# Output projection moved from a stage of its own into the attention loop of a Trainium2 kernel

## What is computed

```python
scores = jnp.einsum('bhqd,bhkd->bhqk', q, k) * scale
scores = jnp.where(causal[None, None], scores, -jnp.inf)
att = jax.nn.softmax(scores, axis=-1)
y = jnp.einsum('bhqk,bhkd->bhqd', att, v)
y = y.transpose(0, 2, 1, 3).reshape(b, t, c)
return y @ Wc                    # the output projection, 256 x 256
...
x = x + _L0_attn_ref(xn, ...) + _L0_ffn_ref(xn, ...)
```

## Time and profile before

| | us |
|---|---|
| median of 3 runs | 2054.63 (2052.05 to 2055.58) |
| profiled execution | 2050.78 |
| its span in the trace | 2049.0 |
| attention's last copy of `pv` ends | 1923.0 |
| `project_out`'s first load issued | 1929.78 |
| last addition ends | 2045.45 |

### The profile page before, as it was taken

The page is one execution under the profiler, slowest core; times in us unless marked ns, Lnnn a source line. Parts: engine busy times, 40 slices in busy tenths (PEclk is TensorE's granted clock), DMA queues, the critical chain, the costliest instruction groups (busy, mean ns, idle before and its releaser), DMA issues. The chain is left out here.

```text
span 2049.0 us, 42600 instructions
## 1 busy us (share of the span) xinstructions
PE 1939.1 (95%) x14289; PEld 733.6 (36%) x14289; DVE 1795.2 (88%) x4744; ACT 1578.8 (77%) x2078; POOL 359.0 (18%) x618
## 2 busy tenths in 40 slices
PE   7899999999699999999999999999999999999698
PEld 6455555555222222222222222222222222222165
DVE  5699999999889999999999989999999999997187
ACT  2566666666089999999899989999999999999500
POOL 0112221111112121221212212122121221211000
PEclk8999999999589999999999999999999999999889
DMA  4133333325411230311303113031130321300376
GB/s 165 42 89 94 99 97 102 86 87 126 91 28 23 32 54 2 54 30 26 54 2 54 31 24 54 2 54 32 24 54 2 53 38 18 54 2 13 101 211 206
DMA packets 146213, 123.32 MB, mean 60 GB/s; under 512 B 82068, under 2 KB 132668, under 8 KB 144572
## 3 DMA queue, kind: packets, MB, share of 16 engines
q1 hardware_dynamic: 137324, 112.55, 25.3%
q10 hardware_dynamic: 8720, 8.65, 1.4%
HBM read 69.50 MB, written 50.86 MB: 59 GB/s over the span
## 5 line engine op out<-in xcount | busy, mean ns | idle before, releaser
L1051 ACT ACTIVATE prob<-st 128x1024 f32<-128x1024 f32 (+3 forms) x1280 | 1071.7, 898 | 83.3 <-PE st L1170 75.4
L1183 PE MATMUL pv<-prob,V 128*32 128x512 f32 (+3 forms) x5120 | 598.6, 542 | 0.1
L1146 PE MATMUL sm<-K,Q 48*128 48x512 f16 (+3 forms) x2176 | 542.1, 350 | 17.0 <-DVE pm L1109 4.7
L1094 DVE CUSTOM_DVE_ANT_0 sm<-sm,mask 128x128 f32<-128x128 f32 (+3 forms) x1024 | 490.5, 510 | 61.1 <-PE sm L1146 53.7
L1109 DVE TENSOR_REDUCE pm<-sm 128x1 f32<-128x512 f32 x768 | 494.6, 685 | 15.0 <-PE sm L1146 12.6
L1170 PE MATMUL st<-Q,K 50*128 50x512 f16 (+3 forms) x2560 | 472.5, 353 | 21.5 <-ACT prob L1051 10.9
L1009 POOL TENSOR_SCALAR_AFFINE_SELECT prob<-prob 128x256 f32<-128x256 f32 x512 | 206.1, 409 | 1116.5 <-ACT prob L1051 1111.4
L1146 PEld LDWEIGHTS sm<-K,Q 48*128 48x128 f16 x2176 | 173.8, 94 | 392.6 <-DVE pm L1109 156.6
L1105 DVE CUSTOM_DVE_ANT_0 sm<-sm,excess 128x512 f32<-128x512 f32 x384 | 264.8, 716 | 25.5 <-PE sm L1146 16.2
L1170 PEld LDWEIGHTS st<-Q,K 50*128 50x128 f16 x2560 | 125.3, 93 | 408.5 <-ACT prob L1051 321.7
L1044 ACT ACTIVATE excess<-st 128x1024 f32<-128x1024 f32 x188 | 190.4, 1032 | 5.1 <-DVE pm L1105 0.7
(11 more groups left out here) (151 smaller groups left out, 1896.2 us busy)
## 6 DMA issues: line engine op xcount, KB each, us to landing
Q<-scratch_q SPq DMA_DIRECT2D x102, 128.0 KB, 4.0
K<-scratch_k SPq DMA_DIRECT2D x102, 128.0 KB, 6.2
x<-in_x SPq DMA_DIRECT2D x18, 512.0 KB, 4.5
scratch_v<-Vs SPq DMA_DIRECT2D x64, 128.0 KB, 2.0
scratch_r<-R SPq DMA_DIRECT2D x16, 512.0 KB, 3.2
V_raw<-scratch_v SPq DMA_DIRECT2D x16, 512.0 KB, 8.8
scratch_y<-Y SPq DMA_DIRECT2D x64, 128.0 KB
Yt<-scratch_y SPq DMA_DIRECT2D x16, 512.0 KB, 5.8
```

The lines of the kernel that those rows point to most:

```text
L1051: act.activation(prob[(slot * UNITS + k) % PT][:, :, 0:width], st[number % ST][:, :, 0:width], ACT.Exp)\
L1094: dve.tensor_tensor_reduce(x, x, mask[:, CH - width:], 1.0, -3e38, ALU.add, ALU.max, pm[:, row, t, k:k + 1]).then_inc(sm_read, 1)
L1146: pe.matmul(dst[:, 0:block_width(t, k)], lhsT=Q[slot][r, h // 2, t * P:(t + 1) * P], rhs=K[slot][r, h // 2, k * CH:k * CH + block_width(t, ...
L1183: i = pe.matmul(pv[2 * DH * h:2 * DH * (h + 1), CH - width:CH], lhsT=V[slot][:, j, h, :], rhs=prob[(slot * UNITS + 2 * n + h // 2) % PT][: ...
```

## The change

`project_out` is gone. Its work goes into `attention`:

- SP moves each half (two chunks, 1024 positions) of Y when it is ready: the four rows of sums to DRAM, and the four heads' y by DMA within the chip's memory into `Yc`, which gathers a batch (`move`).
- The sums come back laid out over 128 partitions x 32 elements (`load_sums`), DVE inverts them there (`invert`), they go to DRAM (`store_inverse`) and come back repeated over 16 partitions a head (`spread_inverse`).
- POOL multiplies `Yc` by them in place, for two quads and one half at a time (`normalise`).
- `SEQ` gets four "project" entries per quad. In quad 4b+i they project chunk i of batch b-1: two fp32 products of 256 columns each, into a bank of the ring `sm`; DVE adds R in place (`add`), SP stores (`store_out`) and loads R for a later chunk (`load_r`). In quads 0 to 3 the entry is a one-column product and a one-column copy.
- The last batch is projected at the end: 8 blocks near the end of the last quad, 8 after it.
- `TIMETABLE` is a new string of 275 symbols for 271, `LEAD` is 7 for 6, V has two buffers for three, and SP's order in a quad is new.

```diff
-LEAD = 6
+LEAD = 7
+PROJECT_AT = (80, 95, 111, 125)
...
+    for s in reversed(range(SUB)):
+        sequence.insert(PROJECT_AT[s], ("project", s))
...
 TIMETABLE = (
-    "ssmmwmmsmswsmmswxmmxmwsmsmmssmwmswsmsmmwxmmsmwmmsmmxmwmmssmmwmmsmsws"
...
+    "smswmmswwsmmsmsmsmmsxxmmwmsmmswmmswwsmsmmwsmmsmsmmmxmmxmwmmsmxmmwsms"
...
+EXTRA = {LATE: NE, **{AHEAD - 2 * (2 * SUB - i) + 1: NE + 1 + i for i in range(2 * SUB)}}
...
+            def move(quad, half):
+                sp.wait_ge(pv_read, quad * TC + 2 * half + 3)
+                t = slice(WIDE * half, WIDE * (half + 1))
+                for h in range(G):
+                    row = 2 * DH * h
+                    sp.dma_start(scr["L"][2 * quad + half, h:h + 1, :], Y[row + DH:row + DH + 1, t]).then_inc(y_moved, 16)
+                for h in range(G):
+                    row, first = 2 * DH * h, G * DH * (quad % 2) + DH * h
+                    sp.dma_start(Yc[quad // QB % 2][first:first + DH, quad % QB // 2, t], Y[row:row + DH, t]).then_inc(y_moved, 16)
+
+            def load_sums(quad, half):
+                k = 2 * quad + half
+                sp.wait_ge(y_moved, 16 + MOVED * (k + 1))
+                sp.dma_start(sums[:, :], L_v[k, :].rearrange("(p j) -> p j", p=P)).then_inc(sums_loaded, 16)
+
+            def store_inverse(quad, half):
+                k = 2 * quad + half
+                sp.wait_ge(inverted, k + 1)
+                sp.dma_start(I_v[k, :].rearrange("(p j) -> p j", p=P), inverse[:, :]).then_inc(inverse_stored, 16)
+
+            def spread_inverse(quad, half):
+                k = 2 * quad + half
+                sp.wait_ge(inverse_stored, 16 * k + 16)
+                if quad >= 2:
+                    sp.wait_ge(normed, 2 * (quad // 2) - 1 + half)
+                for h in range(G):
+                    first = G * DH * (quad % 2) + DH * h
+                    sp.dma_start(spread[half][first:first + DH, :], scr["I"][k, h:h + 1, :].to_broadcast([DH, WIDE])).then_inc(inverse_spread, 16)
...
             def body(quad, slot, last):
+                if quad:
+                    move(quad - 1, 1)
+                load_m(quad, slot, 1)
+                if quad:
+                    load_sums(quad - 1, 1)
                 if not last:
                     sp.wait_ge(pair_used, quad * PAIRS + PT // 2)
                     nxt = (slot + 2) % SLOTS
                     load_qk(sp, scr, (quad + 2) % NQ, Q[nxt], K[nxt], qk_loaded[nxt])
                     sp.wait_ge(v_placed, quad + 1)
                     load_v(quad + 1)
-                load_m(quad, slot, 1)
+                if quad:
+                    store_inverse(quad - 1, 1)
+                    spread_inverse(quad - 1, 1)
+                move(quad, 0)
+                load_sums(quad, 0)
                 load_m(quad, slot, 2, last)
+                store_inverse(quad, 0)
+                spread_inverse(quad, 0)
+                if quad >= TC:
+                    store_out(quad - TC)
+                    load_r(quad - TC + 2)
                 if not last:
                     load_m(quad + 1, (slot + 1) % SLOTS, 0)
...
+            quads(body)
+            move(NQ - 1, 1)
+            load_sums(NQ - 1, 1)
+            store_inverse(NQ - 1, 1)
+            spread_inverse(NQ - 1, 1)
+            for g in range(NCH - TC, NCH):
+                store_out(g)
+                if g + 2 < NCH:
+                    load_r(g + 2)
...
+            def normalise(quad, half):
+
+                pool.wait_ge(inverse_spread, 16 * G * (2 * quad + half + 1))
+                y = Yc[quad // QB % 2][:, quad % QB // 2, WIDE * half:WIDE * (half + 1)]
+                pool.tensor_tensor(out=y, in0=y, in1=spread[half][:, :], op=ALU.mult).then_inc(normed, 1)
...
+                    if n == SUB * (TC - 1) * TC // 2 and quad and quad % 2 == 0:
+                        normalise(quad - 1, 1)
+                    if n == SUB * (TC - 1) * TC // 2 + SUB + 2 and quad % 2:
+                        normalise(quad, 0)
...
+            def invert(k):
+
+                dve.wait_ge(sums_loaded, 16 * k + 16)
+                dve.reciprocal(inverse[:, :], sums[:, :]).then_inc(inverted, 1)
+
+            def add(quad, slot, e, g, s):
+
+                x = sm[(slot * NE + e) % SM]
+                dve.wait_ge(sm_ready, quad * NE + e + 1)
+                if g < 0:
+                    dve.tensor_copy(idle[:, :], x[:, 0:1]).then_inc(sm_read, 1)
+                    return
+                dve.wait_ge(r_loaded, 16 * g + 16)
+                dve.tensor_tensor(out=Rt[g % 2][:, s, :], in0=Rt[g % 2][:, s, :], in1=x[:, 0:C], op=ALU.add).then_inc(sm_read, 1)
...
+                pe.wait_ge(wc_loaded, 16)
+                pe.wait_ge(normed, normed_for(g))
+                t = CH * (g % TC) + P * s
+                for a in range(CC):
+                    i = pe.matmul(dst[:, 0:C], lhsT=Yc[g // TC % 2][:, a, t:t + P], rhs=Wc[:, a, :], start=a == 0, stop=a == CC - 1)
+                i.then_inc(sm_ready, 1)
...
-def project_out(nc, io, w, scr):
...
-        attention(nc, w, scr)
-        project_out(nc, io, w, scr)
+        attention(nc, io, w, scr)
```

More of the change, by code:

```diff
@@ L738 @@
 SLOTS = 3
+VSLOTS = 2
 UNITS = sum(2 * G * (c + 1) for c in range(TC))
@@ L780 @@
 KD = len(QROWS) * DH
+PROJECTS = [next(e for e in range(NE) if SEQ[e] == ("project", s)) for s in range(SUB)]
+INVERT_EARLY, INVERT_LATE = LATE + 2, PROJECTS[2] + 1
+WIDE = 2 * CH
 AHEAD = 75
@@ L873, in attention @@
         Vr = sb("V_raw", [P, T // P, G * DH])
-        V = [sb(f"V{i}", [P, T // P, G, 2 * DH]) for i in range(SLOTS)]
+        V = [sb(f"V{i}", [P, T // P, G, 2 * DH]) for i in range(VSLOTS)]
         prob = [sb(f"prob{i}", [P, 2, CH]) for i in range(PT)]
@@ L884, in attention @@
         mask = sb("mask", [P, CH], bf16)
+        Yc = [sb(f"Yc{i}", [P, CC, T]) for i in range(2)]
+        spread = [sb(f"spread{i}", [P, WIDE]) for i in range(2)]
+        sums = sb("sums", [P, G * WIDE // P])
+        inverse = sb("inverse", [P, G * WIDE // P])
+        Wc = sb("Wc", [P, CC, C])
+        Rt = [sb(f"Rt{i}", [P, SUB, C]) for i in range(2)]
+        idle = sb("idle", [P, 1])
         st = [ctx.enter_context(nc.psum_tensor(f"st{i}", [P, 2, CH], fp32)) for i in range(ST)]
@@ L948, in body @@
                     load_v(quad + 1)
-                load_m(quad, slot, 1)
-                load_m(quad, slot, 2, last)
+                if quad:
[3 more added lines that the diff above has]
+                load_sums(quad, 0)
+                load_m(quad, slot, 2, last)
+                store_inverse(quad, 0)
[3 more added lines that the diff above has]
+                    load_r(quad - TC + 2)
                 if not last:
                     load_m(quad + 1, (slot + 1) % SLOTS, 0)
[L953 to L960, removed]
+            grant(sp, (pv_read, 1), (y_moved, 16), *[(m_loaded, ROWS_LOADED)] * NG)
             load_v(0)
@@ L1012, in body @@
                 assert d == DIAG
-            for s in range(SLOTS):
+            for s in range(VSLOTS):
                 pool.memset(V[s][:, :, :, DH:2 * DH], 1.0)
@@ L1135, in fill @@
                 dst = sm[(slot * NE + e) % SM]
+                if e > NE or e < NE and SEQ[e][0] == "project":
+                    g, s = (quad - TC, SEQ[e][1]) if e < NE else (NCH - TC + (e - NE - 1) // SUB, (e - NE - 1) % SUB)
+                    project(dst, g, s)
+                    return
                 if e == NE or SEQ[e][0] == "rows":
@@ L1372, in build @@
+            for i in range(2 * SUB, TC * SUB):
+                fill(NQ - 1, (NQ - 1) % SLOTS, NE + 1 + i)
 def build(nc, io):
```

197 lines of the change are left out of this document (61 added, 136 removed).

## The result

| | us |
|---|---|
| before, median of 4 runs | 2055.11 (2052.05 to 2060.95) |
| after, median of 4 runs | 1997.88 (1993.09 to 2003.47) |
| ratio | 0.972 (95% interval 0.969 to 0.975) |
| predicted | 2016 (1990 to 2041) |
| profiled execution after, its span | 1996.59, 1994.6 |

The change is 2.8% faster. The sign and the range held; 18 us of gain came on top of the forecast. They are several errors, partly against each other.

A forecast was written before the change was run, and what follows sets the result against it. PE was taken to bound a loop near balance. The span 2049.0 - 92.0 + 41.8 + 6.8 + 4.8 - 4.8 + 4.5 = 2010.1 us, plus the offsets from span to median, gave 2016 us, range 1990 to 2041.

The forecast's parts named there:

- Removal and tail: End of kernel: the old projection stage's 126.0 us go, a tail of 34.0 us comes instead, net -92.0.
- So I take 1.71 a block, 13.7 us for eight: Tail: the eight projection blocks after the pause run with PE's clock at 0.5, 13.7 us in all.
- PE in the loop: Quads 4 to 14: four projection blocks at 0.95 us each, 3.8 us a quad paid almost in full, +41.8.
- rival B: Loop: blocks fill PE's idle time, costing 1.3 to 2.5 us a quad for 3.8; 1995 us, chance 0.18.
- Quads 1 to 3: Near 85.5 us each; growing as much as quads 4 to 14 would mean SP's chain costs, not PE.
- Last quad: Four blocks at 3.8 us, eight more near its end at 3.0 beyond PE's idle time: +6.8, bounds 3 and 12.
- Chunk 2's rows: SP's queue: these rows go ahead of Q, K and V, so PE's waits for them end, -4.8 us.
- one-column entries: Quads 0 to 3: four one-column blocks at 0.3 us, 1.2 us a quad, +4.8, bounds 0 and 6.
- DVE's wait: First half's inversion: sums back at 44.2, wanted at 44.6; for estimate errors 0.3 us on 15 quads, +4.5.
- 132 now, plus the longer blocks: 44.1: Loop: chunk 3's rows are split 44.1 us after the last copy, against 38.0 before with 119 symbols.
- SP's chain: Dependent transfers ahead of chunk 3's rows: V issued at 24.2, spreading 34.5, sums issued 41.9 and back at 44.2 us.
- Rival D: SP's chain later still, delaying chunk 3's rows and scores: 3.0 to 3.5 us gives no change, 6 gives 2095; chance 0.05.

The follow-up runs named there:

- experiment 5: The changed kernel with the old table plus four project symbols, chunk 3's rows issued earlier and the first half's inversion 20 entries later: 2027.55 us, 0.988 of before.
- experiment 8: The changed kernel with the first half's inversion six blocks later and the last batch's first eight blocks in the tail's pause: 1985.57 us, 0.967 of before.
- experiment 9: The kernel of experiment 8 with four 128 x 128 products for each one-column product in quads 0 to 3: 1987.57 us.
- experiment 3: The kernel before with only the new table, less its four project symbols, and LEAD 7: 2077.93 us, 1.011 of before.
- experiment 6: The last batch's first eight blocks moved into the tail's pause: 1992.79 us on the changed kernel, 2019.63 us on the kernel of experiment 5.
- experiment 4: The kernel before with only chunk 2's maxima rows issued ahead of Q, K and V: 2047.8 us, 0.996 of before.
- experiment 7: The changed kernel with only DVE's inversion of a quad's first half six entries later: 1993.28 us, 0.971 of before.

## Why the prediction was right in sign and 18 us high

**Removal and tail (predicted −92.0, measured −97.2).** The chain was right: 15.1 us for 15.6, with POOL at 2.35 for 2.7. The step that failed is "So I take 1.71 a block, 13.7 us for eight": the clock was back after 3 us, and from the start of the first block to the end of the last addition the tail took 10.4 us, not 14.1. The old stage's 20 us at half clock were carried over whole to another stretch. The pause ahead does not tell the two apart, 13.17 us there and 15.71 here; but there PE came back in pieces, with 4.03 us of standing between them, and here it worked without a break:

```profile
1935.55 3.75 PE L1348 MATMUL pr<-rl,E 16*128 16x512 f32 x4 [13.17 <-DVE rl L1296]
1943.32 3.77 PE L1348 MATMUL pr<-rl,E 16*128 16x512 f32 x4 [4.03 <-DVE rl L1296]
```

No run varied this alone, so the reason stays open.

**PE in the loop (predicted +41.8 for quads 4 to 14, measured +24.3, waits included).** Two steps failed, against each other. First, "PE work put in is paid almost in full": by experiment 5 that is so in the old order, where the price of 3.8 us was of the right kind and too small (4.9 measured, 4.6 of it PE's own busy time). In the new order the blocks' work costs 0.8 (experiments 8 and 9). This is rival B's mechanism, stronger than B took it. Second, the prediction gave the reordering itself no price. It costs 1.4 to 1.6 us a quad, in all of them (86.03 and 86.21 in experiments 8 and 3, for 84.6). With the 0.8 that makes the 86.8 of a quad without a late sum. Eleven such quads are 24 us over before; the late sums add 3.8 and chunk 2's rows take off 4.6. That the total came within 1% of the forecast is luck in part: a price too high on the blocks and none on the order went against each other. That PE has 2 us idle says little about the price: the order decides how much idle time there is and whether the blocks fall into it.

**Quads 1 to 3 (predicted near 85.5 us each, measured 86.2, 90.6, 89.1).** The prediction named this as a sign of error: "a quad growing in quads 1 to 3 as much as in 4 to 14 (then SP's chain, not PE, costs)". They grew more, 4.0 us each against 2.2. The reading in the brackets was too narrow: 1.5 us of it is the order, 1.6 DVE's wait in two of them, and three drops of the clock. The one-column entries (+4.8 forecast) cost nothing: 86.03 us with them in experiment 8, 86.21 without them in experiment 3. That holds for the new order; in the old one they cost 2.2 us a quad (experiment 5).

**Last quad (predicted +6.8, measured +12.6).** The failed step is "7.6 us of PE against the 4.6 idle there, so 3.0". Eight blocks cost 7.4 to 7.8 us (experiments 6 and 8): PE's idle time there is spent in waits for ACT, and ACT's idle time in the quad rose from 4.7 us to 14.6, so the two pay in turns. The other 4.8 us are the four loop blocks and the order; 3.8 was forecast. In the old order the last quad with the four blocks alone took 79.4 us (experiment 6), just the 3.8 over 75.6. In the new one most of it seems to be the order: an estimate of 4 us, from the 6.0 of experiment 3, of which a drop of 6.8 us may be 2.0 as in experiment 9. The upper bound given, 12, was passed.

**Chunk 2's rows (−4.8)**: −4.6 in experiment 4, two drops of the clock included. **DVE's wait (+4.5)**: a wait of 1.1 to 1.6 us in five quads, 7 us in sum; without them the median is 4.6 us lower in experiment 7, though the two intervals overlap. The size came out near, but not the reason: the step that failed is "132 now, plus the longer blocks: 44.1". The split came at +42.6 and DVE wanted the sums at +43.0, which fits blocks that cost less than forecast (132 symbols at the old pace alone are 42.2); so the margin of 0.4 us was none. **SP's chain**: forecast within 0.6 us at every hop but the issue of Q, K and V, which came 1.0 to 1.4 earlier. Rival D's further step (chunk 3's rows late) did not come. **Rival E**: the new MATMULs stand at 0.22 us (7.17 us for 32 in experiment 8, and in the earlier trace rows), so the weight loads are hidden.

The Trainium skill's rule that a load overlaps running matmuls only where the row groups differ (TensorE: Matmul & The Clock Gate, "Part 3: Packing small matmuls", The mechanism) does not hold for this shape; the same section also lets loads into a background weight buffer go ahead, and no run here shows which buffer was used. The Trainium skill's rule that each DMA engine takes the descriptors of a ring in order (DMA: Bandwidth & Descriptors, "Queues, rings and completion order") agrees with the store of the inverse in quad 10: it landed 0.7 us behind V, 11.09 us after its issue.

What stays open: which of the new order's moved symbols cost its 1.6 us, and why the same order then takes real blocks for 0.8. The traces show that PE's idle time first rises from 2.1 to 4.2 us and is then filled down to 1.3, not what opens it.

## What to carry to other kernels

Price an insertion into a hand-ordered loop as two terms, what the new order costs without the work and what the work costs in that order, and measure them apart: here they were +1.5 and +0.8 us a quad, where the old order would have asked 4.9. Where two engines alternate and one of them has no work to spare, as at the end of the last quad, the idle time seen on the other is no room; look for a pause in which both stand (here 15 us that took eight blocks for nothing). Work out a queue's chain of dependent hops one by one against the moment at which the consumer comes: the chain came out to within half a microsecond at its end, the consumer's moment only to 1.6, and that was enough for a wait in a third of the rounds.

## What the runs showed of the hardware

- **A loop with less PE work had more stretches at half clock.** With the blocks in place (1.3 us of PE idle a quad) the loop had two or three stretches of 3.4 us at 0.50, with empty entries (3.4 us idle) twelve, and 2009.95 us for 1997.88 (with longer waits for the sums as well). In experiment 3 each cost 1.2 to 1.5 us. In the two places shown PE had stood 0.59 and 1.01 us shortly before. With the new order alone there were five in the loop's full quads; with the old order and blocks two. So idle time alone does not tell how many come, and the count differs from run to run. What sets them off is not shown.
- **How soon the clock came back differed.** After 15.7 us of standing PE ran at half clock for 3.0 us, in the second profile of the same kernel for 3.4, in experiment 8 after only 8.88 us of standing for 5.2; the old stage had stayed there for 20 us, with PE busy for only half of that time.
- **A small store pays for the large loads ahead of it at its issue.** A 16 KB store that was issued right behind twelve loads of 128 KB and V's 512 KB took 6.71 us to issue and 10.84 to land. In the last quad, which has no such loads, the same store took 0.35 and 1.43 us.
